# A 12-sublayer transformer on one core: the attention mask moves from TensorE into VectorE's row minimum, and exp reads SBUF

## The reference

```python
# L2: 4 x 256 tokens in the original shape, H = 16 heads, HD = 16
scores = einsum('bhqd,bhkd->bhqk', q, k) / sqrt(16)
scores = where(causal, -inf, scores)          # causal = key later than query
ctx = einsum('bhqk,bhkd->bhqd', softmax(scores), v) ; out = ctx @ Wo.T + bo
# L3: H = 16 heads, D_HEAD = 128
scores = einsum('bhse,bhme->bhsm', q, k) / sqrt(128)
scores = where(causal, -1e9, scores)
z = einsum('bhsm,bhme->bhse', softmax(scores), v) ; out = einsum('bhse,hde->bsd', z, W_O)
```

## Time and profile before

| | us |
|---|---|
| median of three runs | 1345.94 |
| lowest, highest | 1343.77, 1351.58 |
| span of the profiled execution | 1345.8 |
| TensorE busy in it | 1180.6 (88%) |
| VectorE busy | 913.1 (68%) |
| GpSimd busy | 660.5 (49%) |
| ScalarE busy | 540.0 (40%) |

### The profile page before, as it was taken

How to read it: one execution, slowest core, us unless ns; L and a number is a source line. 1 busy time by engine, 2 the same in 40 slices (tenths; PEclk the granted TensorE clock), 3 DMA queues, 4 the chain that set the end, 5 groups by cost and what they waited for, 6 DMA issues and landing times.

```text
span 1345.8 us, 21983 instructions
## 1 busy us (share of the span) xinstructions
PE 1180.6 (88%) x6937; PEld 996.3 (74%) x6937; DVE 913.1 (68%) x2088; ACT 540.0 (40%) x1225; POOL 660.5 (49%) x784
## 2 busy tenths in 40 slices
PE   6887478999788998979989989997799999999996
PEld 4765266877567787867767778786588887788885
DVE  5578777588878747477768764647666666666666
ACT  3254742210110223237747732321355554455552
POOL 5455726720453386854414458688344443343430
PEclk9788878999889999999999999999799999999998
DMA  5114022220000032322101213223110111011100
GB/s 170 58 49 146 24 77 59 87 86 1 1 1 28 30 105 78 100 64 46 39 19 44 61 45 97 90 86 117 32 48 26 44 27 44 24 40 31 39 8 32
DMA packets 31973, 74.10 MB, mean 55 GB/s; under 512 B 7136, under 2 KB 10464, under 8 KB 31456
## 3 DMA queue, kind: packets, MB, share of 16 engines
q1 hardware_dynamic: 29520, 70.43, 17.5%
q10 hardware_dynamic: 1872, 2.74, 0.6%
q0 software_dynamic: 512, 0.07, 0.0%
HBM read 63.64 MB, written 3.28 MB: 50 GB/s over the span
## 4 chain that ended last, share of the span: by engine, by line
PE 58%; DVE 22%; ACT 9%; issue 6%; POOL 3%; DMA 1%; SPq 0%; DVEq 0%; POOLq 0%; ACTq 0%
PE ps L229 18%; PE ps L231 16%; PE ps L230 16%; DVE a_ptl L1277 4%; ACT a_p L1225 3%; PE ps L1256 3%; DVE small L1204 2%; DVE x L1003 2%; ACT a_pth L1272 1%; DVE ffn_hl L704 1%; ACT ffn_hh L663 1%; DVE d_eq L1831 1%; DVE xn L283 1%; DVE ffn_hf L700 1%; PE ps L329 1%
## 5 line engine op out<-in xcount | busy, mean ns | idle before, releaser
L1243 POOL TENSOR_SCALAR a_p<-a_p,small 128x128 f32<-128x128 f32 (+3 forms) x256 | 132.3, 536 | 280.8 <-DVE small L1234 280.8
L229 PE MATMUL ps<-xh,wh 128*128 128x512 f32 x480 | 198.9, 414 | 9.7 <-POOL wl L420 5.2
L230 PE MATMUL ps<-xl,wh 128*128 128x512 f32 x480 | 192.9, 402 | 0.0
L231 PE MATMUL ps<-xh,wl 128*128 128x512 f32 x480 | 192.8, 402 | 0.0
L1225 ACT ACTIVATE a_p<-ps,small 128x128 f32<-128x128 f32 (+3 forms) x256 | 133.4, 526 | 96.5 <-DVE small L1217 55.8
L389 POOL TENSOR_TENSOR wl<-raw,wh 128x384 fp32r<-128x384 f32 (+2 forms) x120 | 157.7, 1314 | 10.0
L387 POOL TENSOR_SCALAR wh<-raw 128x384 fp32r<-128x384 f32 (+2 forms) x120 | 75.1, 626 | 161.6 <-PE ps L231 161.5
L1277 DVE TENSOR_TENSOR a_ptl<-ps,a_pth 128x384 fp32r<-128x384 f32 (+1 forms) x192 | 106.4, 596 | 53.3 <-ACT a_pth L1272 53.1
L663 ACT ACTIVATE ffn_hh<-ffn_hf 128x512 fp32r<-128x512 f32 x88 | 55.5, 631 | 184.5 <-DVE ffn_hf L698 121.0
L229 PE MATMUL ps<-wh,ffn_hh 128*128 128x256 f32 x352 | 106.4, 302 | 18.7 <-DVE ffn_hl L704 18.7
L420 POOL TENSOR_TENSOR wl<-raw,wh 128x512 fp32r<-128x512 f32 x88 | 119.1, 1354 | 7.3
(11 more groups left out here) (314 smaller groups left out, 3229.6 us busy)
## 6 DMA issues: line engine op xcount, KB each, us to landing
raw<-in_w SPq DMA_DIRECT2D x56, 448.0 KB, 3.3
raw<-in_w SPq DMA_DIRECT2D x32, 384.0 KB, 3.0
raw<-in_qk SPq DMA_DIRECT2D x16, 512.0 KB, 3.6
raw<-in_v SPq DMA_DIRECT2D x16, 256.0 KB, 2.6
delta_table<-d_back SPq DMA_DIRECT2D x4, 528.0 KB, 4.3
d_back<-delta_table ACTq DMA_DIRECT2D x2, 1024.0 KB, 6.4
a_sq<-a_qh SPq DMA_DIRECT2D x64, 32.0 KB, 2.0
a_sk<-a_kh SPq DMA_DIRECT2D x64, 32.0 KB, 2.0
```

Source lines behind the costliest of these rows:

```text
L229: pe.matmul(o, l[0], r[0], start=start, stop=False, skip_group_check=True)
L230: pe.matmul(o, l[0], r[1], start=False, stop=False, skip_group_check=True)
L231: return pe.matmul(o, l[1], r[0], start=False, stop=stop, skip_group_check=True)
L1243: g.tensor_scalar(pp, pp, h_inv[:, par, i:i + 1], 1.0, ALU.mult, ALU.mult).then_inc(sem("at_norm"), 1)
```

## The change

- `pe_scores` has no mask product. It writes `KEYS[i]` columns, so the first tile 128 in place of 256, and waits for the minimum of the previous head's tile (`at_nmx`) in place of its exp (`at_exp`).
- `dve_min` uses one instruction, `tensor_tensor_reduce`: it adds `maskrow` (zeros, and the mask with its sign turned in the last 128 columns), writes the sum to `a2_p` or `a3_p` in SBUF, and gives the row minimum. In the loop it also counts a semaphore, `dve_turn`.
- `act_exp` reads and writes that tensor in place.
- Units 20 and 21 now use `dve_min` too; `dve_max` and its scaling go. The scale, with its sign turned, moves into both halves of q (`act_fill` with a scale, `dve_fill` with a scale).
- The constants change: `maskrow` in place of two bf16 masks, and no bf16 identity; TensorE's first transposes wait for the identity's load itself.

```diff
-                if positive(n * TT - TT + max(i, 1) + 1):
-                    pe.wait_ge(sem("at_exp"), n * TT - TT + max(i, 1) + 1)
+                if positive(n * TT - TT + max(i, 1) + 1):
+                    pe.wait_ge(sem("at_nmx"), n * TT - TT + max(i, 1) + 1)
                 bank, at = S_AT[i]
-                o = ps[:, bank, at:at + S_COLS[i]]
+                o = ps[:, bank, at:at + KEYS[i]]
                 if isinstance(q(i), tuple):
-                    mm3(pe, o, q(i), k(S_COLS[i]), True, False)
+                    last = mm3(pe, o, q(i), k(KEYS[i]), True, True)
                 else:
-                    pe.matmul(o, q(i), k(S_COLS[i]), start=True, stop=False, skip_group_check=True)
-                pe.matmul(ps[:, bank, at + i * P:at + (i + 1) * P], identb[:, :], mask or maskb[:, :], start=False, stop=True,
-                          skip_group_check=True).then_inc(sem("at_s"), 1)
+                    last = pe.matmul(o, q(i), k(KEYS[i]), start=True, stop=True, skip_group_check=True)
+                last.then_inc(sem("at_s"), 1)
...
+        def dve_min(v, n, par, p, groups=((0, 1), (2,), (3,))):
             for tiles in groups:
                 v.wait_ge(sem("at_s"), tiles[-1] + 1 + n * TT)
+                if not isinstance(n, int):
+                    v.sem_inc(sem("dve_turn"), 1)
                 for i in tiles:
                     bank, at = S_AT[i]
-                    v.tensor_reduce(h_nmx[:, par, i:i + 1], ps[:, bank, at:at + KEYS[i]], AX_X, ALU.min)\
-                        .then_inc(sem("at_nmx"), 1)
+                    v.tensor_tensor_reduce(p[:, par, P_AT[i]:P_AT[i + 1]], ps[:, bank, at:at + KEYS[i]],
+                                           maskrow[:, T - KEYS[i]:T], 1.0, -NEG, ALU.add, ALU.min,
+                                           h_nmx[:, par, i:i + 1]).then_inc(sem("at_nmx"), 1)
...
-                s.activation(p[:, par, P_AT[i]:P_AT[i + 1]], ps[:, bank, at:at + KEYS[i]], ACT.Exp,
+                s.activation(p[:, par, P_AT[i]:P_AT[i + 1]], p[:, par, P_AT[i]:P_AT[i + 1]], ACT.Exp,
...
-            if bias is None:
+            if scale is not None:
+                ins = v.scalar_tensor_tensor(out=dst, in0=ps[:, bank, 0:cols], scalar=scale, in1=f32(hi),
+                                             op0=ALU.mult, op1=ALU.subtract)
+            elif bias is None:
...
-                        one(("q", hh, 0), a3_qh[:, :])
+                        one(("q", hh, 0), a3_qh[:, :], scale=-SCALE3)
...
-                        dve_max(v, n + (hh + 1), 1 - hh, SCALE3)
+                        dve_min(v, n + (hh + 1), 1 - hh, a3_p)
...
-            v.wait_ge(sem("ident_in"), 16)
-            v.tensor_copy(identb[:, :], ident[:, :]).then_inc(sem("const_ident"), 1)
```

More of the change, by code:

```diff
@@ L169, in build @@
         rinv = small[:, 308:312]
-        h_sum, h_inv, h_max, h_nmx = [small[:, 400 + 8 * k:408 + 8 * k].rearrange("p (h i) -> p h i", h=2) for k in range(4)]
+        h_sum, h_inv, h_nmx = [small[:, 400 + 8 * k:408 + 8 * k].rearrange("p (h i) -> p h i", h=2) for k in range(3)]
         idx8 = sb("idx8", [P, TT, 8], U32)
@@ L318, in pe_T @@
             b = u % 2
-            pe.wait_ge(sem("const_ident"), 1)
+            pe.wait_ge(sem("ident_in"), 16)
             pe.wait_ge(sem("ln_xn"), TT * (u + 1))
@@ L1181, in build, with pe_scores @@
         A3_FILL = {20: 2 * (4 + 3 * H), 21: 2 * (4 + 3 * H) + 7 * H}
-        def pe_scores(pe, n, q, k, mask=None):
+        def pe_scores(pe, n, q, k):
             for i in range(TT):
                 if positive(n * TT - TT + max(i, 1) + 1):
-                    pe.wait_ge(sem("at_exp"), n * TT - TT + max(i, 1) + 1)
+                    pe.wait_ge(sem("at_nmx"), n * TT - TT + max(i, 1) + 1)
                 bank, at = S_AT[i]
-                o = ps[:, bank, at:at + S_COLS[i]]
+                o = ps[:, bank, at:at + KEYS[i]]
@@ L1272, in act_fill, with dve_fill @@
             s.activation(dst, ps[:, bank, 0:cols], func, **how).then_inc(sem("at_fhi"), 1)
-        def dve_fill(v, fill, bank, dst, hi, cols=T, bias=None):
+        def dve_fill(v, fill, bank, dst, hi, cols=T, bias=None, scale=None):
             v.wait_ge(sem("at_fhi"), fill + 1)
-            if bias is None:
+            if scale is not None:
+                ins = v.scalar_tensor_tensor(out=dst, in0=ps[:, bank, 0:cols], scalar=scale, in1=f32(hi),
+                                             op0=ALU.mult, op1=ALU.subtract)
+            elif bias is None:
                 ins = v.tensor_tensor(dst, ps[:, bank, 0:cols], f32(hi), ALU.subtract)
@@ L1319, in scores @@
                 pe_scores(pe, n0 + h,
-                          lambda i: a2_sq[:, h % 2, i * P:(i + 1) * P], lambda n: a2_sk[:, h % 2, 0:n], maskp[:, :])
+                          lambda i: a2_sq[:, h % 2, i * P:(i + 1) * P], lambda n: a2_sk[:, h % 2, 0:n])
             scores(0)
@@ L1396, in dve_att2 @@
                         ins.then_inc(sem("a2_vlo"), 1)
-            dve_min(v, n0, 0)
+            dve_min(v, n0, 0, a2_p)
             dve_rinv(v, n0, 0)
@@ L1404, in dve_att2 @@
                 if h + 1 < H:
-                    dve_min(v, n0 + h + 1, (h + 1) % 2, ((0, 1), (2,), (3,)) if h == 0 else ((2,), (3,)))
+                    dve_min(v, n0 + h + 1, (h + 1) % 2, a2_p, ((0, 1), (2,), (3,)) if h == 0 else ((2,), (3,)))
                 if h == 8:
@@ L1411, in dve_att2 @@
                     if f == 1 and h + 2 < H:
-                        dve_min(v, n0 + h + 2, h % 2, ((0, 1),))
+                        dve_min(v, n0 + h + 2, h % 2, a2_p, ((0, 1),))
                     lo, hi = pt_cols(f)
@@ L1559, in pair, with one @@
                 base, n = f0 + 2 + r * BODY, r * 2 + n0
-                def one(key, dst, cols=T):
-                    act_fill(s, base + fills[key][0], fills[key][1], dst, cols)
+                def one(key, dst, cols=T, **how):
+                    act_fill(s, base + fills[key][0], fills[key][1], dst, cols, **how)
                 for f in range(2):
@@ L1574, in pair @@
                     if not done:
-                        act_exp(s, n + (hh + 1), 1 - hh, SCALE3, a3_p)
+                        act_exp(s, n + (hh + 1), 1 - hh, -1.0, a3_p)
                     one(("z", hh, 0), a3_zh[:, :])
-            act_fill(s, f0, 2, a3_qh[:, :])
+            act_fill(s, f0, 2, a3_qh[:, :], scale=-SCALE3)
             act_fill(s, f0 + 1, 0, a3_kh[:, :])
-            act_exp(s, n0, 0, SCALE3, a3_p)
+            act_exp(s, n0, 0, -1.0, a3_p)
             pair(0)
@@ L1592, in pair, with one @@
                 base, n = f0 + 2 + r * BODY, r * 2 + n0
-                def one(key, dst, src, cols=T):
-                    dve_fill(v, base + fills[key][0], fills[key][1], dst, src, cols)
+                def one(key, dst, src, cols=T, scale=None):
+                    dve_fill(v, base + fills[key][0], fills[key][1], dst, src, cols, scale=scale)
                 for f in range(2):
@@ L1602, in pair @@
                     if not done:
-                        one(("q", hh, 0), a3_ql[:, :], a3_qh[:, :])
+                        one(("q", hh, 0), a3_ql[:, :], a3_qh[:, :], scale=-SCALE3)
                         one(("k", hh, 0), a3_kl[:, :], a3_kh[:, :])
@@ L1613, in pair @@
                         dve_stats(v, u + 1)
-            dve_fill(v, f0, 2, a3_ql[:, :], a3_qh[:, :])
+            dve_fill(v, f0, 2, a3_ql[:, :], a3_qh[:, :], scale=-SCALE3)
             dve_fill(v, f0 + 1, 0, a3_kl[:, :], a3_kh[:, :])
-            dve_max(v, n0, 0, SCALE3)
+            dve_min(v, n0, 0, a3_p)
             dve_rinv(v, n0, 0)
@@ L1927, in dve_consts @@
             v.wait_ge(sem("const_in"), 16 * CONSTS)
[L1928 to L1929 removed]
+            v.memset(maskrow[:, 0:T - P], 0.0).then_inc(sem("const_mask"), 1)
+            v.tensor_scalar(maskrow[:, T - P:T], maskcol[:, :], -1.0, None, ALU.mult).then_inc(sem("const_mask"), 1)
             v.tensor_scalar(att_cols[:, 0:DC], att_cols[:, 0:DC], -SCALE2, None, ALU.mult).then_inc(sem("const_mask"), 1)
```

6 lines of the change are left out of this document (1 added, 5 removed).

## The result

The changed kernel takes 1332.13 us (median of 4 runs, 1331.51 to 1333.00), the kernel before 1345.05 us beside it (4 runs, 1343.77 to 1351.58): a ratio of 0.9905, interval 0.9884 to 0.9926, so about 13 us less. That is inside the range of the prediction and 5.5 us under its number, nearly where the rival of a free second result stood (1331.9). The profiled execution took 1331.98 us, its span is 1330.2 us.

A forecast was written before the change was run, and what follows sets the result against it. TensorE was taken to bound units 20/21, a VectorE and ScalarE ring units 14/15. Terms: -15.0 - 1.2 + 0.2 + 7.7 = -8.3 us from 1345.9, giving 1337.6 us; range 1330 to 1352.

The forecast's parts named there:

- a free second result: Rival: the new VectorE instruction's second output costs below 0.03 us; -14.0 us, 1331.9 us; chance 0.17.
- Part 1: Four mask products a head leave TensorE, first tile smaller: -15.0 us in units 20/21, -1.2 at starts of 14/15.
- Part 2: TensorE's score banks wait for the minimum instead of exp; nothing waited for exp, so 0.
- Part 3: VectorE's minimum becomes add, write and minimum: four times the extra, 0.24 us a head in units 14/15, 28 rounds.
- e: Extra time of VectorE's new instruction over the plain minimum, taken as 0.06 us.
- The draining: Rival: the second result drains VectorE, extra 0.1 to 0.2 us; at 0.14 +0.7 us, 1346.6 us; chance 0.2.
- the scan's rate: Rival: the four minima of each round stream at the scan's rate; +21 us, 1367 us; chance 0.06.
- Part 4: ScalarE's exp reads SBUF instead of PSUM: 0.035 us a round in units 14/15, only one exp counted.
- the ring: Units 14/15: a head is a cycle of VectorE and ScalarE alone, 4.55 us a plain round, TensorE beside it.
- Part 5: Units 20/21: dropped scalings and other VectorE and ScalarE work run beside TensorE with 1.0 us of slack; nothing added.
- Saving not kept: Rival: something else closes the pair in units 20/21, so TensorE's saving is lost; 1352.6 us; chance 0.04.
- The clock in units 14 and 15: Rival: the granted clock falls there as TensorE idles 1 us or more a round; tens of us; chance 0.03.

The follow-up runs named there:

- experiment 1: Kernel before the change with only its mask products left out (no causal mask computed): 1331.72 us, ratio 0.9901.
- experiment 7: Next unit's LayerNorm statistics pieces spread in the first pair of units 20 and 21: with old-form units 14/15 1331.31 us, on the changed kernel alone 1331.43 us.
- experiment 5: Changed kernel with units 14 and 15 put back to their form before the change, units 20 and 21 kept new: 1333.72 us, ratio 0.9918.
- experiment 3: Changed kernel with TensorE's score banks waiting for exp again: 1337.20 us first, then 1334.69 us beside the changed kernel itself at 1334.47.
- experiment 4: Changed kernel with exp reading scores from PSUM, banks released by exp, zeros for the mask: 1331.62 us, ratio 0.9896.
- experiment 6: Changed kernel with one extra minimum over 256 keys a head: in units 14 and 15 alone 1343.51 us, in units 20 and 21 alone 1336.23 us.
- the second of experiment 6: Changed kernel with one extra minimum over 256 keys a head in units 20 and 21 alone: 1336.23 us, ratio 0.9943.
- experiment 2: Changed kernel with mask products back on TensorE and zeros in the row VectorE adds: 1345.37 us, ratio 0.9997.
- the first of 7: Units 20/21 new, 14/15 old, with the next unit's LayerNorm statistics pieces spread in the first pair of units 20 and 21: 1331.31 us, ratio 0.9899.

## Why the prediction was right, and the term that was mis-sized

**Part 1, masks off TensorE: right in mechanism and size, wrong in the count.** I had 0.50 us a head (0.48 and 0.02) for 30 heads, 15.0 us. Measured 0.52 to 0.53 in 24 heads (experiment 1: 0.50 for the masks alone) and 0.42 in the last but one of each unit; units 20 and 21 together gave 13.8. The first head of each unit keeps nothing of it, since the LayerNorm statistics hold its chain (experiment 7): its 0.16 is not there in experiment 1, which has only the masks off. The last head of unit 20 became 0.44 us longer, and the stretch from it to the next unit another 0.45, both with the clock at the lower level. I looked for the places where the chain leaves TensorE at the end of a unit only the earlier trace rows; it does at the beginning as well. The starts of units 14 and 15 were put at 1.0 from masks; experiment 1 shows 1.9 with scatter in it, and going back in experiment 5 left a gain of 1.1 of the 2.2 us of rounds, so they cost about 1.1.

**Part 2, the release: right.** Nothing that shows, by two kernels run beside each other (experiment 3).

**Part 3, e: here lies the error, the term that was mis-sized.** I took 0.06 us for the second result, from the index search, whose second part starts 0.06 behind its first. Measured: 0.01 in the chain for each instruction. The accumulator read exists, as the two-instruction form foresaw, but it starts together with whatever comes next. The three minima of a round took 0.04 us more (0.56 + 0.48 against 0.53 + 0.47), not 4 x 0.06 = 0.24; and as the minimum of 512 hardly grew, it didn't enter the chain, so three count and not four. The draining and the scan's rate fell with it: 687 ns at 512, against the 0.8 us named as the limit and the scan's 1205.

The Trainium skill, VectorE: DVE Perf Modes, section Two Vector instructions with no wait between them, says that an operation that also writes out its accumulator is two instructions. This trace agrees: 256 reads of 84 ns stand beside 256 main instructions. By the page one knows that there are two, not that the second costs 0.01 us.

**Part 4, exp from SBUF: right for one exp, wrong in the count.** 0.025 and 0.027 us for the two exps of the ring (714 against 689 ns, 608 against 581), a little under the 0.035 that I read from the earlier trace rows. But both exps count, 0.05 a round in the chain and about 0.04 by experiment 4, just because the minimum of 512 stayed out: the two errors hang together, as the rival of the free result had it (28 x 0.070 = 2.0). Parts 3 and 4 were 7.7 us over 28 rounds; measured 0.08 x 28 = 2.2. That is 5.5 us of cost too much, against 1.2 us of gain too much in units 20 and 21 (15.0 for 13.8): with both put right the sum is about -12.6, where -8.3 was forecast and -12.7 traced. Most of the rest of the distance from 1337.6 to 1332.1 is the median of before, 0.9 us lower beside the kernel after than the 1345.9 that I started from. The two errors had opposite signs, so the number was nearer than its terms.

**Part 5: right in the middle heads.** They stay with TensorE even with 0.33 us more on VectorE (experiment 6), so the slack I read from the earlier trace rows is there. At the ends of the units it isn't, and so my 0 for the dropped scaling was wrong there. Before the change it is a piece of the chain of unit 20's last head, 0.30 us with the waits around it:

```profile
1131.23 0.18 DVE small L1217
```

Without it, and with 0.08 us more in the four exps, the last head of unit 21 came down by 0.19 us with no mask in the chain.

**The rivals.** *Free second result*: this happened. The bound of e under 0.03 held with 0.01. *Saving not kept*: out, 26 heads kept it. *The clock in units 14 and 15*: 1.00 over the windows, although TensorE waits longer there. The windows leave out the starts of the two units, where it is at 0.50 for some us before the change as after it (from 607 to 610 us in both kernels). And in two kernels, the one of experiment 4 and the second of experiment 6, it fell in the middle of unit 15; of experiment 4:

```profile
748.00:751.00 3.00, 3.00 (x15) 3.00 (x14) 1.93 (x8) 1.58 (x6) 1.23 (x4) 0.50 0.17 38
```

There the chain goes to TensorE for a while; the step takes 6.52 instead of 5.66 us, and the next is 0.18 shorter. So what this rival feared exists, at 0.7 us a time and not at tens. It came in two of the nine traces without masks in these units and in none of the four with them, which is too few to tell.

**What the profile was to show.** No mask product, a TensorE-bound window, 0.5 us less a head, two instructions for each minimum, exp 0.03 us longer: all seen. A plain round of 4.8 us: it is 4.62. Exp of 512 started by the minimum: no, its idle time before it is 0.0.

## What to carry to other kernels

The same edit is a gain where the engine it relieves carries the chain and a cost where the engine it loads does; cost it for each stage by that stage's chain, and count heads at both ends of a unit apart, where other work stands in the queue. When a price is missing, ask whether the extra instruction holds up the next one or runs beside it: take the distance from start to start, not the duration. A median over a few runs could not tell 1 to 3 us here. The steps in the traces could, to 0.01 us, except where the granted clock fell, so add up whole units before calling a shorter step a gain.

## What the runs showed of the hardware that I had not expected

VectorE's accumulator read takes 84 ns by itself and delays the next VectorE instruction by about 0.01 us: from one minimum to the next it is 0.21 us (643.78 to 643.99) for 128 keys where it was 0.20 with the plain minimum (645.64 to 645.84).

At the end of unit 20 the granted clock falls. The chain of the kernel after, behind 2.00 us in which TensorE waited for z's low half, and the window over it:

```profile
1126.59 0.12 PE ps L227
...
1126.84 0.21 PE ps L229
```

```profile
1127.00:1130.00 3.00, 2.82 (x14) 2.42 (x12) 0.15 (x1) 0.74 (x2) 2.92 (x3) 0.50 0.00 0
```

0.50 is the lower of the two levels, 1.2 GHz, and the products take 0.21 us instead of 0.12. TensorE had been busy until 1124. It waits there in the kernel before too, for 1.66 us, at 1.00 throughout. It fell at this place in every trace without mask products in units 20 and 21 (the kernel after, experiments 1 and 3 to 7), where the wait is 1.86 to 2.33 us, and not in experiment 2, which has them and waits 1.54 us. So the shorter heads come with a longer wait. That alone doesn't decide it: the wait of 2.00 us at the end of unit 21 in the kernel after left the clock at 1.00, while in three other traces the clock fell there as well (experiment 1, the second kernel of 6, the first of 7). What brings it on was not tried and stays open. In the kernel after it cost the last head of unit 20 some 0.6 us (9.18 against 8.55 in unit 21, where the pieces stayed short) and the stretch behind it 0.45; in the same kernel again the step was 9.71.
